# Causal attention on one core: four heads weighed in a row, diagonal masks in quarters of the array

## The chip, the cores and the metric

One core of a Trainium2 chip runs the whole program. The time is the device time of one execution, in microseconds; the time of a kernel is the median of its runs. The kernel before ran three times: 2082.1, 2084.21 and 2092.12 us, median 2084.21.

## What is computed

The reference has four layers on an input `x` of 4 batches by 1024 positions by 128: window attention (stage a in the kernel), gated linear attention with routes (stage b), causal attention with a short-term memory (stage c), and a mixture of experts (stage d). The change is in stage c alone. Of that stage, cut to the part that matters:

```python
B, L, D, H = (4, 1024, 128, 16); d = 8      # 16 heads of 8 columns
scores = jnp.einsum('bhid,bhjd->bhij', q, k) * scale
causal_mask = jnp.triu(jnp.full((Ll, Ll), -10000.0, dtype=scores.dtype), 1)
attn = jax.nn.softmax(scores + causal_mask, axis=-1)
y_softmax = jnp.einsum('bhij,bhjd->bhid', attn, v)
# a scan over positions gives y_stp; a gate mixes y_softmax and y_stp
```

## The kernel before, in words

**Units and items.** Stage c (`causal`, L990) works on units: one batch and one group of four heads, 16 units in all. Every engine walks the same list of items, written by a planner, `causal_order` (L855), and takes from it what is its own. The kinds that matter here are these.

- `M` (L1092): scores with query rows on the output's 128 partitions, for two heads at a time in the two halves of a two-bank PSUM buffer. VectorE takes the row maxima of them (L1261). A unit has 20 M.
- `S` (L1113): the negative maxima, turned, which then go into the operands of the next kind.
- `W` (L1120): the scores again, key rows on the partitions, the maxima already subtracted, for two heads (index `i` is the pair, `r` the head in it). ScalarE makes the weights from them with one exponential (L1375) into one of four SBUF buffers `c_probs`. A unit has 12 steps (`KEY_STEPS`, a chunk of 512 queries by 128 key rows) and so 24 W.
- `V` (L1139): weights times values (8 columns and a column of ones) for the two heads of one W, accumulated in one of two PSUM banks `acc`. Its matmuls are float32, with 9 output columns each; head `h` writes partitions from `32 * h` on, so the four heads of a group use four 32-column strips of the array. A unit has 24 V.
- `A` copies a finished chunk out of `acc` (L1381).

**Masks.** A tile of scores that holds a part of the diagonal gets the mask added by the array: a matmul of a scaled unit matrix (`half_rows`) with a matrix of 0 and -100 (`causal_row` for M, L1106 to L1111; `causal_col` for W, L1131 to L1137). Each constant is stored on 64 rows, twice, since the operands of the two heads lie in rows 0 to 63 and 64 to 127. A mask matmul reads 64 rows and writes all 128 output partitions; the first pair of matmuls serves output partitions 0 to 63 and adds zeros to the others, the second pair the other way round. So a diagonal pair of score matmuls is followed by four mask matmuls, of 128, 128, 64 and 64 columns (M) or 64, 64, 128 and 128 (W).

**What sets the order.** The scores of M, S and W and some side items share three PSUM buffers in turn (`ring`); PE waits for a buffer until the engine that reads its last content is done (`pe_wait_free`, L1010). The planner keeps a clock for PE, ScalarE and VectorE, with a price for each kind of item (`times`, L911). It puts W and V in their fixed order and lets M of later units go ahead of them where PE would not be held up (`put_ahead`, L960). V of a W is put three W later (`late`, L978). ScalarE's exponential into a buffer waits for the V that read this buffer four W before (L1374). Side items (the next batch's preparation, the short-term memory's scans, which take VectorE, ScalarE and POOL, and the finish of the batch before) are hung on fixed steps.

**Stages a and b** also appear in the rows: L500 and L524 are stage a's scores (up to 64 rows by 64 columns of the array), L459 its masks (64 by 64), L540 its values: 16 float32 matmuls for a block, in four 32-column strips and two halves of 64 rows. L1063 is stage c's first gate matmul, two matmuls into the same 64 columns. L1910 and L1864 are two groups of stage b with 64 and 128 output columns.

Of the kernel before, what the change touches and what calls it, by code (L numbers as in the profile page):

```python
# [13 lines left out]
P = 128  # L14
BANK = 512
EPS = 1e-5
HEADS, HD = 16, 8
# [47 lines left out]
def constant_columns():  # L65
# [13 lines left out]
        "half_rows": np.concatenate([r % 64 == c, r % 64 + 64 == c], 1) * 100.0,  # L79
# [37 lines left out]
def build(nc, x_in, packed, x_out, place, batches, T, known):  # L117
# [7 lines left out]
    with ctx:  # L125
# [729 lines left out]
        def causal_order():  # L855
# [55 lines left out]
            def times(item):  # L911
# [4 lines left out]
                if item[0] in "WV":  # L916
# [3 lines left out]
                    if item[0] == "V":  # L920
                        return 0.02 + 0.00103 * cols, (), 0
# [7 lines left out]
            def begin(item):  # L929
                t = clock["P"]  # L930
                if times(item)[2]:
                    t = max(t, free[0])
                return max(t, made[item[1:]]) if item[0] == "V" else t
# [36 lines left out]
            for u in units:  # L970
                for k, (c, j) in enumerate(KEY_STEPS):
                    for i in range(2):
# [17 lines left out]
        def causal():  # L990
# [49 lines left out]
            def pe_program():  # L1040
# [3 lines left out]
                for item in order:  # L1044
# [47 lines left out]
                    elif kind == "M":  # L1092
# [6 lines left out]
                        for i in range(per):  # L1099
                            pair = (g * GROUP + h0) // 2 + i  # L1100
                            o = [ps[:, r * BANK + i * width:r * BANK + (i + 1) * width] for r in range(2)]
                            for r in range(2):
                                mm = nc.tensor.matmul(o[r], qs[half(r, SCORE), pair, n * P:(n + 1) * P],  # L1103
                                                      ks[half(r, SCORE), pair, a:c], start=True, stop=not diag)
# [15 lines left out]
                    elif kind == "W":  # L1120
# [7 lines left out]
                        for r in range(2):  # L1128
                            mm = nc.tensor.matmul(ps[:, r * BANK:r * BANK + cols], ks[half(r, SHIFT), pair, j * P:(j + 1) * P],  # L1129
                                                  qs[half(r, SHIFT), pair, a:a + cols], start=True, stop=not diag)  # L1130
                        if diag:  # L1131
                            for r in range(2):
                                nc.tensor.matmul(ps[:, r * BANK:r * BANK + 64], w3["half_rows"][half(r, 64), 0:P],
                                                 w3["causal_col"][half(r, 64), 0:64], start=False, stop=False)
                            for r in range(2):
                                mm = nc.tensor.matmul(ps[:, r * BANK:r * BANK + P], w3["half_rows"][half(r, 64), P:2 * P],  # L1136
                                                      w3["causal_col"][half(r, 64), 64:64 + P], start=False, stop=True)  # L1137
                        mm.then_inc(c_key_scored.up(item), 1)
                    elif kind == "V":  # L1139
                        _, b, g, c, j, i = item  # L1140
# [6 lines left out]
                        if j == 0 and i == 0 and ci >= 2:  # L1147
# [1476 lines left out]
```

## Time and profile before

| what | value |
|---|---|
| median of three runs | 2084.21 us |
| the profiled execution's own time | 2081.97 us |
| its span | 2080.6 us |
| mean granted PE clock | 0.936 |
| instructions | 45291 |
| stage c | about 1058 to 1775 us |

A row of the profile names the line, the engine, the operation and the tiles, with the shape of a matmul as rows*columns of the stationary operand and the moving operand's partitions x columns. `busy` counts the time in which at least one such instruction is shown at work.
### The profile page before, as it was taken

Reading aid. Unit: us, or ns where it says so; the run is one execution under the profiler, and the core shown is the slowest. Engines: PE = TensorE matmul, PEld = TensorE weight load, DVE = VectorE, ACT = ScalarE, POOL = GpSimd, SP = SyncE. Lnnn points to the kernel's source line nnn. Section 1 sums busy time; section 2 is a strip of 40 time slices with the busy share of each in tenths; the row PEclk is TensorE's granted clock in tenths of the full one; section 3 lists DMA queues with packets and bytes.
Section 4 is the critical chain, followed back from the end, with each engine's and each line's share of the span. In section 5 each row is a group of like instructions: output and inputs, shape, how many; then the busy total and the mean of one; then the engine's idle time right before and its main releaser. Section 6 shows DMA issues by size and latency. Waiting matters only on the chain.

```text
span 2080.6 us, 45291 instructions
## 1 busy us (share of the span) xinstructions
PE 1812.6 (87%) x19452; PEld 1056.7 (51%) x19472; DVE 1295.3 (62%) x2096; ACT 1134.7 (55%) x1720; POOL 660.3 (32%) x468
## 2 busy tenths in 40 slices
PE   4688879999999999999658899799889988598799
PEld 2456646776677677677522324233333423355465
DVE  5566536666666666666566776586677663555544
ACT  2365647667666766766315676566566665222221
POOL 5220004342343434235504442544444344000000
PEclk8899969999999999999858999899999999799999
DMA  6754000000000000000161532252262220000000
GB/s 166 215 132 96 7 9 1 2 1 1 2 2 1 1 2 2 1 2 2 73 148 42 161 77 50 88 137 63 82 143 62 62 63 21 0 11 6 6 11 11
DMA packets 38361, 102.08 MB, mean 49 GB/s; under 512 B 3856, under 2 KB 12176, under 8 KB 34704
## 3 DMA queue, kind: packets, MB, share of 16 engines
q1 hardware_dynamic: 38160, 99.18, 18.5%
q8 instruction: 153, 2.51, 0.5%
q14 instruction: 48, 0.39, 0.1%
HBM read 66.93 MB, written 31.46 MB: 47 GB/s over the span
## 4 chain that ended last, share of the span: by engine, by line
PE 56%; DVE 20%; issue 8%; ACT 5%; POOL 4%; DMA 1%; POOLq 0%; DVEq 0%; SPq 0%; ACTq 0%
PE accs L1153 8%; DVE arena L1261 4%; PE ring L1870 3%; PE accs L1934 3%; PE ring L2364 3%; PE ring L2366 3%; PE accs L2333 3%; PE ring L1896 3%; PE ring L1129 2%; PE ring L1103 2%; DVE arena L1271 2%; PE ring L1864 2%; PE ring L1835 2%; DVE arena L2023 1%; DVE arena L2063 1%
## 5 line engine op out<-in xcount | busy, mean ns | idle before, releaser
L1261 DVE TENSOR_REDUCE arena<-ring 128x2 f32<-128x1024 f32 (+2 forms) x320 | 346.1, 1112 | 148.1 <-PE ring L1110 97.2
L1375 ACT ACTIVATE arena<-ring 128x1024 f32<-128x1024 f32 (+3 forms) x384 | 304.3, 808 | 174.4 <-PE ring L1136 139.0
L1153 PE MATMUL accs<-arena 128*9 128x512 f32 (+3 forms) x1536 | 322.2, 500 | 0.0
L1129 PE MATMUL ring<-arena 51*128 51x512 bf16 (+3 forms) x768 | 133.5, 342 | 26.7 <-DVE arena L1261 14.8
L1103 PE MATMUL ring<-arena 48*128 48x512 bf16 (+3 forms) x768 | 131.5, 353 | 22.7 <-DVE arena L1261 10.0
L2248 POOL TENSOR_TENSOR arena<-arena 128x1280 f32<-128x1280 f32 x28 | 65.3, 2332 | 265.2 <-PE accs L1934 234.6
L1129 PEld LDWEIGHTS ring<-arena 51*128 51x128 bf16 x768 | 37.9, 94 | 207.0 <-issue 82.9
L2240 POOL TENSOR_TENSOR arena<-arena 128x512 f32<-128x512 f32 x112 | 138.9, 1272 | 10.2 <-DVE arena L2044 10.2
L2232 POOL TENSOR_TENSOR arena<-arena 128x1024 f32<-128x1024 f32 x32 | 75.6, 2364 | 190.2 <-DVE arena L2063 190.2
L2443 DVE TENSOR_TENSOR arena<-arena,ring 128x512 f32<-128x512 f32 x80 | 55.0, 688 | 122.7 <-PE ring L2366 112.2
L2493 ACT ACTIVATE arena<-ring 128x512 f32<-128x512 f32 x80 | 47.8, 597 | 147.0 <-PE ring L2364 147.0
L1538 POOL TENSOR_TENSOR arena<-arena 128x1024 f32<-128x1024 f32 x28 | 65.9, 2352 | 190.5 <-ACT arena L1388 147.9
L294 PE MATMUL ring<-weights_constants,xn 128*128 128x128 f32 x124 | 35.4, 379 | 84.1 <-DVE xn L278 52.6
L1271 DVE TENSOR_TENSOR_SCAN arena<-arena 128x1024 f32<-128x1024 f32 x32 | 79.5, 2484 | 34.5 <-POOL arena L1526 34.5
L2333 PEld LDWEIGHTS accs<-weights_large,arena 128*128 128x128 f32 x640 | 85.1, 193 | 29.2 <-issue 26.3
L2063 DVE TENSOR_TENSOR arena<-ring,arena 128x1024 f32<-128x1024 f32 x32 | 39.2, 1225 | 85.9 <-PE ring L1896 85.9
L1896 PE MATMUL ring<-arena 64*128 64x128 f32 x1024 | 91.7, 285 | 0.2
L1896 PEld LDWEIGHTS ring<-arena 64*128 64x128 f32 x1024 | 79.2, 187 | 19.5 <-issue 12.9
L2159 ACT ACTIVATE arena<-ring 128x1024 f32<-128x1024 f32 x32 | 32.8, 1024 | 100.7 <-PE ring L1835 100.7
L1996 DVE SCALAR_TENSOR_TENSOR arena<-ring,arena 128x1024 f32<-128x1024 f32 x32 | 39.2, 1225 | 76.0 <-ACT arena L2163 76.0
L1103 PEld LDWEIGHTS ring<-arena 48*128 48x128 bf16 x768 | 38.3, 97 | 94.9 <-issue 34.8
L2333 PE MATMUL accs<-weights_large,arena 128*128 128x128 f32 x640 | 85.0, 276 | 1.5 <-DVE arena L2449 0.5
(334 smaller groups left out, 4365.5 us busy)
## 6 DMA issues: line engine op xcount, KB each, us to landing
arena<-whole_k SPq DMA_DIRECT2D x32, 512.0 KB, 4.6
arena<-whole_q SPq DMA_DIRECT2D x32, 512.0 KB, 6.2
arena<-a_scratch_q SPq DMA_DIRECT2D x16, 384.0 KB, 6.9
arena<-a_scratch_k SPq DMA_DIRECT2D x16, 384.0 KB, 8.3
arena<-c_scratch_q SPq DMA_DIRECT2D x16, 384.0 KB, 8.2
arena<-c_scratch_k SPq DMA_DIRECT2D x16, 384.0 KB, 10.1
a_scratch_k<-arena SPq DMA_DIRECT2D x8, 512.0 KB, 3.9
c_scratch_k<-arena SPq DMA_DIRECT2D x8, 512.0 KB, 5.2
```

Of the source, the lines that this page charges most:

```text
L1103: mm = nc.tensor.matmul(o[r], qs[half(r, SCORE), pair, n * P:(n + 1) * P], ks[half(r, SCORE), pair, a:c], start=True, stop=not diag)
L1129: mm = nc.tensor.matmul(ps[:, r * BANK:r * BANK + cols], ks[half(r, SHIFT), pair, j * P:(j + 1) * P], qs[half(r, SHIFT), pair, a:a + cols] ...
L1153: mm = nc.tensor.matmul(acc[ci % 2][32 * h:32 * h + HD + 1, a - c * BANK:BANK], c_values[b % 2][:, j, r * HEADS // 2 + 2 * g + i, :], weig ...
L1261: nc.vector.tensor_reduce(dst, src, AX.X, ALU.max, negate=True).then_inc(c_max_taken.up(item), 1)
L1271: nc.vector.tensor_tensor_scan(sk[:, :], c_retain[:, j:j + 1].to_broadcast([P, T]), sk[:, :], 0.0, ALU.mult, ALU.add).then_inc(c_state_mad ...
L1375: nc.scalar.activation(view(c_probs[wi % 4]), view(ps), ACT.Exp).then_inc(c_weights_made.up(item), 1)
L1538: nc.gpsimd.tensor_tensor(sq[:, :], sk[:, :], sq[:, :], ALU.mult).then_inc(c_y_step.up((b, j)), 1)
L1896: mm = nc.tensor.matmul(ps[:, r * BANK + p * P:r * BANK + (p + 1) * P], k_[t % 2][half(r), p * P:(p + 1) * P], q_[t % 2][half(r), p * P:(p ...
L2232: nc.gpsimd.tensor_tensor(masked[0][:, :], masked[0][:, :], masked[1][:, :], ALU.add).then_inc(gla_joined.up(t), 1)
L2240: nc.gpsimd.tensor_tensor(pair_cols(q2m[t % 2][:, r, :]), pair_cols(q2[t % 2][:, :]), hot_b[:, r * P:(r + 1) * P].unsqueeze(1).to_broadcas ...
L2248: nc.gpsimd.tensor_tensor(state_mid[:, :, :, :].rearrange("p a r d -> p (a r) d"), state[:, :, :, :].rearrange("p a r d -> p (a r) d"), fa ...
L2333: mm = nc.tensor.matmul(total[:, n * P:(n + 1) * P], hid[index[item] % 3][:, n * P:(n + 1) * P], w("d_down", f * P, (f + 1) * P), start=f ...
```

## The change

It does four things. In the planner, and in PE's program, a V is one item for all four heads of a step: its eight records follow each other, and it waits for the weights of both pairs. It is put behind both W of the next step (the list `late` holds one step). Its planned price is 0.00205 us per column in place of two items of 0.02 + 0.00103 per column. Each mask matmul writes only the 64 output partitions that it is for: a 64-column stationary operand and an output of 64 partitions, four matmuls for the four pairs of input half and output half. Waits of other engines on V are on the one item.

```diff
-        "half_rows": np.concatenate([r % 64 == c, r % 64 + 64 == c], 1) * 100.0,
+        "half_rows": (r % 64 == c[:, 0:64]) * 100.0,
...
-                        return 0.02 + 0.00103 * cols, (), 0
+                        return 0.00205 * cols, (), 0
...
-                return max(t, made[item[1:]]) if item[0] == "V" else t
+                return max(t, made[item[1:] + (1,)]) if item[0] == "V" else t
...
-                        late.append(("V", *u, c, j, i))
-                        if len(late) > 3:
-                            item = late.pop(0)
-                            put_ahead(item)
-                            put(item)
-                            if item[4:] == ((item[3] + 1) * BANK // P - 1, 1):
-                                sums.append(("A", *item[1:4]))
+
+                    late.append(("V", *u, c, j))
+                    if len(late) > 1:
+                        item = late.pop(0)
+                        put_ahead(item)
+                        put(item)
+                        if item[4] == (item[3] + 1) * BANK // P - 1:
+                            sums.append(("A", *item[1:4]))
...
                             if diag:
-                                for r in range(2):
-                                    nc.tensor.matmul(o[r][:, width - P:width], w3["half_rows"][half(r, 64), 0:P],
-                                                     w3["causal_row"][half(r, 64), 0:P], start=False, stop=False)
-                                for r in range(2):
-                                    mm = nc.tensor.matmul(o[r][:, width - 64:width], w3["half_rows"][half(r, 64), P:2 * P],
-                                                          w3["causal_row"][half(r, 64), P:P + 64], start=False, stop=True)
+
+                                for h, first, cols in ((0, width - P, slice(0, P)), (1, width - 64, slice(P, P + 64))):
+                                    for r in range(2):
+                                        mm = nc.tensor.matmul(o[r][half(h, 64), first:width], w3["half_rows"][half(r, 64), 0:64],
+                                                              w3["causal_row"][half(r, 64), cols], start=False, stop=True,
+                                                              skip_group_check=True)
...
                         if diag:
-                            for r in range(2):
-                                nc.tensor.matmul(ps[:, r * BANK:r * BANK + 64], w3["half_rows"][half(r, 64), 0:P],
-                                                 w3["causal_col"][half(r, 64), 0:64], start=False, stop=False)
-                            for r in range(2):
-                                mm = nc.tensor.matmul(ps[:, r * BANK:r * BANK + P], w3["half_rows"][half(r, 64), P:2 * P],
-                                                      w3["causal_col"][half(r, 64), 64:64 + P], start=False, stop=True)
+                            for h, last, columns in ((0, 64, slice(0, 64)), (1, P, slice(64, 64 + P))):
+                                for r in range(2):
+                                    mm = nc.tensor.matmul(ps[half(h, 64), r * BANK:r * BANK + last],
+                                                          w3["half_rows"][half(r, 64), 0:64], w3["causal_col"][half(r, 64), columns],
+                                                          start=False, stop=True, skip_group_check=True)
...
-                        pe.wait_ge(c_weights_made, ("W", *item[1:]))
-                        weights = c_probs[w_index["W", b, g, c, j, i] % 4]
-                        for r in range(2):
-                            h = 2 * i + r
-                            mm = nc.tensor.matmul(
-                                acc[ci % 2][32 * h:32 * h + HD + 1, a - c * BANK:BANK],
-                                c_values[b % 2][:, j, r * HEADS // 2 + 2 * g + i, :],
-                                weights[:, r * BANK:r * BANK + (c + 1) * BANK - a],
-                                start=j == 0, stop=j == (c + 1) * BANK // P - 1, skip_group_check=True)
+                        pe.wait_ge(c_weights_made, ("W", *item[1:], 1))
+                        for i in range(2):
+                            weights = c_probs[w_index["W", b, g, c, j, i] % 4]
+                            for r in range(2):
+                                h = 2 * i + r
+                                mm = nc.tensor.matmul(
+                                    acc[ci % 2][32 * h:32 * h + HD + 1, a - c * BANK:BANK],
+                                    c_values[b % 2][:, j, r * HEADS // 2 + 2 * g + i, :],
+                                    weights[:, r * BANK:r * BANK + (c + 1) * BANK - a],
+                                    start=j == 0, stop=j == (c + 1) * BANK // P - 1, skip_group_check=True)
...
-                            ac.wait_ge(c_weighed, ("V", *w_items[wi - 4][1:]))
+                            ac.wait_ge(c_weighed, ("V", *w_items[wi - 4][1:5]))
```

## Rows read from the trace of the kernel before

**Rows 1.** The page: busy time of each engine over the span.

```profile
PE 1812.6 (87%) x19452; PEld 1056.7 (51%) x19472; DVE 1295.3 (62%) x2096; ACT 1134.7 (55%) x1720; POOL 660.3 (32%) x468
```

**Rows 2.** Stretches of the causal stage; columns are named in the first line.

```profile
core 0: us, PE busy (x) PEld busy (x) DVE busy (x) ACT busy (x) POOL busy (x), PEclk, DMA share, GB/s
1058.00:1089.00 31.00, 19.44 (x172) 8.66 (x172) 26.70 (x28) 1.01 (x1) 3.32 (x5) 0.50 0.42 85
1089.00:1144.00 55.00, 48.01 (x398) 15.99 (x398) 38.18 (x51) 29.57 (x38) 21.23 (x18) 0.80 0.22 52
1300.00:1352.00 52.00, 40.95 (x322) 14.77 (x318) 30.38 (x31) 27.77 (x33) 29.88 (x22) 0.87 0.28 86
1352.00:1404.00 52.00, 49.21 (x508) 16.89 (x502) 41.82 (x37) 33.28 (x44) 21.99 (x14) 1.00 0.60 139
1404.00:1456.00 52.00, 50.53 (x478) 20.07 (x476) 36.13 (x42) 32.45 (x45) 21.67 (x17) 1.00 0.26 63
1612.00:1664.00 52.00, 51.51 (x506) 21.30 (x502) 35.68 (x43) 32.43 (x45) 20.92 (x13) 1.00 0.25 62
1089.00:1760.00 671.00, 610.62 (x5530) 219.29 (x5531) 448.27 (x478) 415.05 (x526) 294.43 (x198) 0.95 0.32 83
```

**Rows 3.** Chain of waits from 1196 to 1248 us, shares by line.

```profile
by line: PE accs L1153 38.1%; PE ring L1129 11.4%; PE ring L1103 10.7%; DVE arena L1261 9.8%; DVE arena L1271 8.5%; issue 7.5%; ACT arena L1375 7.4%; PE ring L1136 1.9%; PE ring L1107 1.9%; PE ring L1117 1.9%; PE ring L1133 1.1%; PE ring L1
```

**Rows 4.** Timeline of PE: start, us, engine, line, operation, out<-in, count.

```profile
1403.71 0.38 PE L1103 MATMUL ring<-arena 48*128 48x512 bf16 x2
1403.93 0.22 PE L1107 MATMUL ring<-bf_causal_row,bf_half_rows 64*128 64x128 bf16 x2
1403.99 0.19 PE L1110 MATMUL ring<-bf_causal_row,bf_half_rows 64*128 64x64 bf16 x2
1404.11 1.03 PE L1153 MATMUL accs<-arena 128*9 128x512 f32 x4
1405.07 0.28 PE L1129 MATMUL ring<-arena 51*128 51x256 bf16 x2
```

**Rows 5.** Groups of L540 (one block), L1063 (two matmuls), L1153 (one block): busy, mean ns.

```profile
L540 PE MATMUL ring<-arena 64*9 64x128 f32 x32 | 0.6, 270 | 0.0
...
L1063 PE MATMUL ring<-xnT,weights_small 128*64 128x512 f32 x4 | 1.9, 605 | 0.0
...
L1153 PE MATMUL accs<-arena 128*9 128x512 f32 x4 | 1.0, 594 | 0.0
```

**Rows 6.** Groups by shape, 1089 to 1760 us: busy us, mean ns | idle before.

```profile
L1153 PE MATMUL accs<-arena 128*9 128x512 f32 x768 | 204.2, 610 | 0.0
...
L1136 PE MATMUL ring<-bf_causal_col,bf_half_rows 64*128 64x128 bf16 x512 | 57.4, 218 | 0.0
L1153 PE MATMUL accs<-arena 128*9 128x384 f32 x256 | 52.5, 488 | 0.0
...
L1153 PE MATMUL accs<-arena 128*9 128x256 f32 x256 | 39.5, 392 | 0.0
L1153 PE MATMUL accs<-arena 128*9 128x128 f32 x256 | 26.3, 288 | 0.0
```

**Rows 7.** Timeline of PE in stages a and b, where the layout changes in columns.

```profile
157.13 0.41 PE L500 MATMUL ring<-arena 48*64 48x128 bf16 x16
157.47 0.65 PE L540 MATMUL ring<-arena 64*9 64x128 f32 x32
158.04 0.41 PE L459 MATMUL ring<-bf_win_col,ident 64*64 64x512 bf16 x4
...
429.22 0.65 PE L1910 MATMUL ring<-arena 128*64 128x256 f32 x4
429.81 0.61 PE L1864 MATMUL ring<-arena 128*128 128x136 f32 x3
```

**Rows 8.** Groups of VectorE and ScalarE, 1089 to 1760 us; idle before them last.

```profile
L1261 DVE TENSOR_REDUCE arena<-ring 128x2 f32<-128x1024 f32 (+2 forms) x295 | 320.7, 1115 | 138.7 <-PE ring L1110 88.0 <-PE ring L1103 49.4
L1375 ACT ACTIVATE arena<-ring 128x1024 f32<-128x1024 f32 (+3 forms) x384 | 304.3, 808 | 174.4 <-PE ring L1136 139.0 <-PE ring L1129 34.2
```

More of the change, by code:

```diff
@@ L1103, in pe_program @@
                                 mm = nc.tensor.matmul(o[r], qs[half(r, SCORE), pair, n * P:(n + 1) * P],
-                                                      ks[half(r, SCORE), pair, a:c], start=True, stop=not diag)
+                                                      ks[half(r, SCORE), pair, a:c], start=True, stop=not diag,
+                                                      skip_group_check=True)
                             if diag:
-                                for r in range(2):
-                                    nc.tensor.matmul(o[r][:, width - P:width], w3["half_rows"][half(r, 64), 0:P],
-                                                     w3["causal_row"][half(r, 64), 0:P], start=False, stop=False)
-                                for r in range(2):
-                                    mm = nc.tensor.matmul(o[r][:, width - 64:width], w3["half_rows"][half(r, 64), P:2 * P],
-                                                          w3["causal_row"][half(r, 64), P:P + 64], start=False, stop=True)
+                                for h, first, cols in ((0, width - P, slice(0, P)), (1, width - 64, slice(P, P + 64))):
+                                    for r in range(2):
+                                        mm = nc.tensor.matmul(o[r][half(h, 64), first:width], w3["half_rows"][half(r, 64), 0:64],
+                                                              w3["causal_row"][half(r, 64), cols], start=False, stop=True,
+                                                              skip_group_check=True)
                         mm.then_inc(c_row_scored.up(item), 1)
@@ L1129, in pe_program @@
                             mm = nc.tensor.matmul(ps[:, r * BANK:r * BANK + cols], ks[half(r, SHIFT), pair, j * P:(j + 1) * P],
-                                                  qs[half(r, SHIFT), pair, a:a + cols], start=True, stop=not diag)
+                                                  qs[half(r, SHIFT), pair, a:a + cols], start=True, stop=not diag,
+                                                  skip_group_check=True)
                         if diag:
-                            for r in range(2):
-                                nc.tensor.matmul(ps[:, r * BANK:r * BANK + 64], w3["half_rows"][half(r, 64), 0:P],
-                                                 w3["causal_col"][half(r, 64), 0:64], start=False, stop=False)
-                            for r in range(2):
-                                mm = nc.tensor.matmul(ps[:, r * BANK:r * BANK + P], w3["half_rows"][half(r, 64), P:2 * P],
-                                                      w3["causal_col"][half(r, 64), 64:64 + P], start=False, stop=True)
+                            for h, last, columns in ((0, 64, slice(0, 64)), (1, P, slice(64, 64 + P))):
[3 more added lines that the diff above has]
+                                                          start=False, stop=True, skip_group_check=True)
                         mm.then_inc(c_key_scored.up(item), 1)
                     elif kind == "V":
-                        _, b, g, c, j, i = item
+                        _, b, g, c, j = item
                         a = first_query(c, j)
@@ L1146, in pe_program @@
                         pe.wait_ge(c_cleared, ("ones", 1))
-                        if j == 0 and i == 0 and ci >= 2:
+                        if j == 0 and ci >= 2:
                             pe.wait_ge(c_copied, ci - 2)
-                        pe.wait_ge(c_weights_made, ("W", *item[1:]))
-                        weights = c_probs[w_index["W", b, g, c, j, i] % 4]
-                        for r in range(2):
-                            h = 2 * i + r
-                            mm = nc.tensor.matmul(
-                                acc[ci % 2][32 * h:32 * h + HD + 1, a - c * BANK:BANK],
-                                c_values[b % 2][:, j, r * HEADS // 2 + 2 * g + i, :],
-                                weights[:, r * BANK:r * BANK + (c + 1) * BANK - a],
-                                start=j == 0, stop=j == (c + 1) * BANK // P - 1, skip_group_check=True)
+                        pe.wait_ge(c_weights_made, ("W", *item[1:], 1))
[8 more added lines that the diff above has]
+                                    start=j == 0, stop=j == (c + 1) * BANK // P - 1, skip_group_check=True)
                         mm.then_inc(c_weighed.up(item), 1)
@@ L1242, in dve_program @@
                         if b >= 2:
-                            dv.wait_ge(c_weighed, ("V", b - 2, GROUPS - 1, *KEY_STEPS[-1], 1))
+                            dv.wait_ge(c_weighed, ("V", b - 2, GROUPS - 1, *KEY_STEPS[-1]))
                         nc.vector.tensor_tensor(
@@ L1377, in act_program @@
                         _, b, g, c = item
-                        ac.wait_ge(c_weighed, ("V", b, g, c, (c + 1) * BANK // P - 1, 1))
+                        ac.wait_ge(c_weighed, ("V", b, g, c, (c + 1) * BANK // P - 1))
                         if b:
```

## The prediction

> **What bounds the kernel now.** I read the page's sums first, then stretches of the causal stage, then the chain, then single matmuls. TensorE is busy for 87% of the span [rows 1], and the change touches one stage only, from about 1058 to 1760 us. From 1089 us on, where key rows are weighed, PE shows 610.6 of 671 us busy, VectorE (DVE) 448 and ScalarE (ACT) 415; in the calm stretches PE shows 50.5 and 51.5 of 52 us at the full clock, near a batch's start 41 [rows 2]. The chain through one calm stretch spends 38% in the weighing matmuls of L1153 [rows 3]. So PE sets the pace there, and the question is how much of it the change frees and what takes over.
>
> A PE row must be read with its tail: a 512-column weighing record lasts 0.594 us, but four of them span 1.03, so the second two started 0.43 after the first two [rows 4, 5]. 0.43 is streaming, 0.16 is drain that the next matmul overlaps. Where neighbours use the array the same way, the next starts when the streaming ends (L1103 at 1403.71, its mask 0.22 later). Where they don't, it starts later: L1110 streams 0.03 from 1403.99 and L1153 begins at 1404.11, 0.09 late; L1153 streams 0.86 from 1404.11 and L1129 begins at 1405.07, 0.10 late [rows 4]. I call this a switch.
>
 Its size: records average 0.610, 0.488, 0.392 and 0.288 us for 512, 384, 256 and 128 columns, each with 0.165 of tail; with 192, 64, 64 and 64 pairs of heads and two record-times per pair, 192x2x0.445 + 64x2x(0.323+0.227+0.123) = 257 us [rows 6]. Half is **128 us** less.
>
> There are also 192 blocks instead of 384. Each now stands alone between scores [rows 4], so 192x(0.09+0.10) = **36 us** less of switching.
>
> **Part 2: masks of 64 output rows.** Now four mask matmuls over 128 output rows follow their scores with no switch and cost 0.06 + 0.03 = 0.09 us (1403.93 to 1403.99, then 0.03) [rows 4]. After, they are quarters of the array: all four stream together, 0.053 us for the longest, half the difference that 128 columns make in the averages of rows 6 (0.104 from 128 to 256, two passes). But the layout now differs from that of the scores (64 rows by 128 columns of the array against 64 by 64). Does a change of columns alone cost a switch? Yes by the nearest rows: from 48*64 to 64*9, L500's streaming ends at 157.13+0.41-0.16 = 157.38 and L540 begins at 157.47; back, L540 ends at 157.96 and L459 begins at 158.04; and from 64 to 128 columns over all rows L1910 ends at 429.71 and L1864 begins at 429.81 [rows 7]. All are 0.08 to 0.10. These bound it: 0 below (if scores and masks pass without a drain), 0.09 above each way. I take 0.09 in and 0.095 out, since no change of layout in these rows was free. There are 512 pairs with a diagonal (256 in M, 256 in W; the 512 records of L1136, two per pair, are W's [rows 6]). 512x(0.053+0.09+0.095-0.09) = 76 us more; where a block of values follows the mask its own switch is already counted, about 125 of the 192 blocks (two steps of three are diagonal): 12 off. Net **64 us** more; with free switches it would be 19 us less.
>
> **Part 3: the later wait.** A block waits for the exponentials of its second score. Behind it in PE's queue stand the next M and W, for which DVE and ACT wait. From that second score to the block PE has one block (0.96), two scores (0.22 to 0.5 each) and most often one or two M: 1.9 to 2.8 us. ACT needs at most two exponentials of 0.81 on average [rows 8], more for 512 columns, and a hand-over: 1.8 to 2.3 us. So the wait is 0 mostly and 0.3 where no M stands between, in the last unit. ACT's wait for a free buffer is for a block that stands two steps back: nothing. The planner's price of four heads (0.00205 per column) is twice its price of two, so it spreads M nearly as before; I cost the new order at 0, between -5 and +10. The narrower constant is loaded and cast in stage a under other work: 0. No DMA is moved, and nothing on SyncE's or POOL's queue.
>
> **The sum.** PE gets 128 + 36 - 64 = **100 us** less work. It can't all show. DVE's 448 us and ACT's 415 [rows 2] would fill 78% and 73% of 571 us, and scores take turns in three PSUM buffers. In the densest stretch DVE has 41.8 of 52 us [rows 2], which would be 95% of a stretch 15% shorter. On the other side, DVE waits 139 us for scores (L1110's and L1103's) and ACT 174 us [rows 8], so both have room, and the block that keeps scores waiting comes half as often at the same length. The calm stretches should give their share nearly whole, the batch starts half of it, and the densest ones less: I take two thirds, 64 us. The profiled execution took 2081.97 us: 2018. The median of the runs shown lies 2.2 above it: **2020 us**.
>
> **A rule against it.** Two heads of 512 columns take 1.03 us [rows 4], two record-times and a tail. The Trainium skill, "TensorE: Matmul & The Clock Gate", Part 3, says that matmuls start and end in program order ("strict FIFO"). By that rule a head's second record would hold back the next head's first: two heads would take three record-times, 1.45 us with the tail. The trace disagrees: they take two.
>
> **The rivals.**
> B, masks switch for free: a gain of 19 in place of a loss of 64, so 183 us of relief, but then DVE binds in more stretches; 95 to 100 us show: 1986. For: masks follow in the same row halves. Against: every change of columns in rows 7 cost 0.09. 13%.
> C, another engine takes over at once: DVE, or the order of three buffers, lets a third through, 33 us: 2051. For: DVE at 41.8 of 52. Against: its waits of rows 8. 14%.
> D, the slower side: four heads don't run together. Place: L1153. If a 512-column block streams 1.72 us (two and two), the 128 us are gone while the masks' 64 stay: 64-36 = 28 us slower, 2112. It decides from about 1.53 us of streaming per 512-column block on, where 128 shrinks to 28. Against: eight at a time in rows 5; for: those read half the rows each, and no row has four full-height streams. The extreme of D is that each head's second record holds back the next head's first: five record-times, 2.15 us where two pairs stream 1.72 now, so 257 us become 321, +64 + 64 - 36 = 92 us slower, 2176. 6% for both, of which 1% for the extreme. That extreme is what the skill's strict order gives; the trace disagrees already at two heads.
> E, the change doesn't do what it says: if the planner's new order or the later wait makes PE stall by 0.33 us at each of the 192 blocks, the 64 us are eaten: 2084. Against: the slack worked out in part 3. 4%.
> F, the clock: PE's granted share is 0.80 to 0.87 in the batch starts and 0.50 in the stretch before [rows 2], where PE sat idle more. If a PE that waits more runs a fifth of its remaining 511 us (611 - 100) at half the clock, 102 us come back: 2122. Against: the calm stretches stay at 1.00 with masks and waits in them. 3%.
>
> **How the numbers follow.** A, the forecast, has 60%, its own range 1995 to 2045 (four to nine tenths of the relief). 0.5% is 10.4 us, about what a measurement can tell from no change. Faster: A+B+C = 0.87; same: E = 0.04; slower: D+F = 0.09. The range takes in A and nearly all of B and C: 1980 to 2055.
>
> **What would show it.** L1153: 192 groups of eight records, 512 columns in about 1.05 us; about 1.9 is rival D. Masks: 64*64, four starts within 0.01 us, 0.09 after the score's streaming ends; no gap is rival B. PE busy in the stage falls below DVE's pace: calm stretches near 44 us for what took 52, with DVE at 85% or more. DVE's wait for PE should shrink from 139 us; if it stays while PE's wait for DVE grows, the ring is the bound (C). Above 2074 I am wrong in kind; below 1980 the masks' price was wrong.

## The result and the profile after

The changed kernel takes 2109.62 us (median of 4 runs, 2107.08 to 2112.47) against 2085.37 for the kernel before. The ratio is 1.0112, with a 95% interval from 1.0082 to 1.0142: **1.1% slower**, clear of the noise, where 3.1% faster was forecast. The range ended at 2055. The profiled execution took 2112.47 us, its span is 2111.2.

The page of the changed kernel: busy times [rows 1], and the slices of the span with the granted clock.

```profile
PE 1817.4 (86%) x19452; PEld 1051.2 (50%) x19472; DVE 1289.1 (61%) x2096; ACT 1130.4 (54%) x1720; POOL 658.2 (31%) x468
...
PEclk8899969999999999999857779769878988799999
```

PE's sum is 5 us more than before. The clock row shows the first surprise: five slices at 7 and one at 6 between 1108 and 1785 us, where the stage changed by this work lies. The page of the kernel before has two slices at 8 there and 9 in all others:

```profile
PEclk8899969999999999999858999899999999799999
```

The stage in one row, from its first W score to its last weighing matmul (columns as in [rows 2]):

```profile
1094.00:1785.00 691.00, 603.63 (x5492) 210.83 (x5492) 436.40 (x467) 408.98 (x523) 286.04 (x196) 0.81 0.32 80
```

The same stage took 662 us before, 1089 to 1751:

```profile
1089.00:1751.00 662.00, 605.29 (x5497) 214.44 (x5498) 441.63 (x468) 414.08 (x524) 288.78 (x196) 0.95 0.33 84
```

The stage is 29 us longer, and PE shows the same 604 us of busy time. But PE got 0.81 of its clock in place of 0.95 (0.815 and 0.952 with one digit more). The granted clock in the traces has two levels, 1.2 and 2.4 GHz, so twice the missing share is the time at 1.2 GHz: 256 us of the stage after, 63 us before.

**Did the four heads run together?** The timeline of PE in two places, the first at the full clock and the second at half (columns as in [rows 4]; the last brackets give a wait and its releaser):

```profile
1618.45 0.23 PE L1131 MATMUL ring<-arena 51*128 51x128 bf16 x2 [0.76 <-DVE arena L1264]
...
1619.87 0.39 PE L1131 MATMUL ring<-arena 51*128 51x512 bf16 x2
1620.19 0.25 PE L1137 MATMUL ring<-bf_causal_col,bf_half_rows 64*64 64x64 bf16 x4
1620.37 0.39 PE L1104 MATMUL ring<-arena 48*128 48x512 bf16 x2
...
1624.21 1.04 PE L1156 MATMUL accs<-arena 128*9 128x512 f32 x8
1625.19 0.28 PE L1131 MATMUL ring<-arena 51*128 51x256 bf16 x2
```

```profile
1404.69 1.90 PE L1156 MATMUL accs<-arena 128*9 128x512 f32 x8
1406.52 0.40 PE L1131 MATMUL ring<-arena 51*128 51x256 bf16 x2
```

Yes: eight records of 512 columns last 1.04 us, where four did before [rows 4]. At half the clock the same block lasts 1.90. A reader who sees only the second row would take it for rival D, four heads in two turns. It isn't: the clock of the stretch tells them apart. The block at 1404.69 lies in a stretch with a granted clock of 0.50 (second row; columns as in [rows 2]):

```profile
1387.00:1391.00 4.00, 4.00 (x42) 2.41 (x38) 0.73 (x4) 0.98 (x4) 0.00 (x0) 0.92 1.01 193
1391.00:1411.00 20.00, 17.45 (x150) 5.03 (x143) 12.87 (x12) 8.05 (x13) 7.98 (x7) 0.50 0.64 136
1411.00:1418.00 7.00, 5.18 (x63) 2.17 (x61) 5.46 (x5) 5.67 (x8) 0.90 (x1) 0.96 0.02 6
```

**Masks.** The score that starts at 1619.87 has streamed its 512 columns (0.22 us) at 1620.09; its masks begin at 1620.19, 0.10 late; the next score begins 0.18 after them. A pair's masks cost 0.28 us of PE, against 0.09 before.

The same by shape, weighing matmuls of the stage (busy us, mean ns, idle before; compare [rows 6]):

```profile
L1156 PE MATMUL accs<-arena 128*9 128x512 f32 x768 | 125.1, 729 | 1.8 <-ACT arena L1378 1.8
...
L1156 PE MATMUL accs<-arena 128*9 128x384 f32 x256 | 32.8, 590 | 0.0
...
L1156 PE MATMUL accs<-arena 128*9 128x256 f32 x256 | 22.8, 432 | 0.0
...
L1156 PE MATMUL accs<-arena 128*9 128x128 f32 x256 | 15.3, 310 | 0.5 <-ACT arena L1378 0.5
```

By the prediction's own formula they stream 96x2x0.564 + 32x2x(0.425+0.267+0.145) = 162 us, from 257. Half would have been 128.5; each record is longer on average, 729 ns for 610, because a part of the blocks ran at half the clock, as the one of 1.90 us did.

VectorE's maxima and ScalarE's exponentials wait more, not less ([rows 8] had 138.7 and 174.4), and PE waits more for the maxima before its W scores: 31.5 us, from 14.8. By the prediction's own sign, this is the ring of three buffers and not PE alone.

```profile
L1264 DVE TENSOR_REDUCE arena<-ring 128x2 f32<-128x1024 f32 (+1 forms) x294 | 321.0, 1115 | 174.5 <-PE ring L1111 99.5 <-PE ring L1104 73.8
L1378 ACT ACTIVATE arena<-ring 128x1024 f32<-128x1024 f32 (+3 forms) x384 | 300.7, 809 | 190.8 <-PE ring L1137 154.4 <-PE ring L1131 34.2
L1131 PE MATMUL ring<-arena 51*128 51x512 bf16 (+3 forms) x768 | 142.1, 376 | 43.2 <-DVE arena L1264 31.5 <-ACT arena L1335 4.7 <-ACT arena L1378 3.1
```

and in the kernel before:

```profile
L1129 PE MATMUL ring<-arena 51*128 51x512 bf16 (+3 forms) x768 | 133.5, 342 | 26.7 <-DVE arena L1261 14.8 <-DVE arena L1244 6.0 <-ACT arena L1332 4.9
```

The chain through a stretch at the full clock, 1612 to 1664 us, was led by the weighing matmuls before (first row) and is led by VectorE after (second row):

```profile
by line: PE accs L1153 41.6%; PE ring L1129 14.4%; DVE arena L1261 8.3%; PE ring L1103 8.0%; PE ring L1164 7.3%; DVE arena L1271 4.2%; PE ring L1180 3.8%; PE ring L1182 3.4%; PE ring L1172 2.8%; PE ring L1136 2.3%; PE ring L1107 1.7%; PE ri
by line: DVE arena L1264 31.1%; PE accs L1156 19.9%; PE ring L1104 9.6%; PE ring L1131 9.5%; DVE arena L1274 8.5%; PE ring L1137 5.5%; PE ring L1167 3.9%; PE ring L1111 3.9%; PE ring L1084 3.7%; PE ring L1078 2.0%; ACT arena L1361 2.0%; iss
```

Every engine waits more for another. That fits a loop better than one bound engine; e9, e10 and e12 below test it.

### The profile page after: what moved, and what is told of

The parts are those of the page before. It is cut to its first block, busy times and chain, and to the rows that moved or that the text cites. A ratio compares the mean times of both kernels' runs of the same rounds, so it can differ in the third digit from the quotient of the medians.

```text
span 2111.2 us, 45102 instructions
## 1 busy us (share of the span) xinstructions
PE 1817.4 (86%) x19452; PEld 1051.2 (50%) x19472; DVE 1289.1 (61%) x2096; ACT 1130.4 (54%) x1720; POOL 658.2 (31%) x468
## 4 chain that ended last, share of the span: by engine, by line
PE 55%; DVE 22%; issue 7%; ACT 4%; POOL 4%; DMA 1%; POOLq 0%; DVEq 0%; SPq 0%
DVE arena L1264 7%; PE accs L1156 5%; PE ring L1873 3%; PE accs L1937 3%; PE ring L2367 3%; PE ring L1104 3%; PE ring L2369 3%; PE accs L2336 3%; PE ring L1131 3%; PE ring L1899 3%; DVE arena L1274 2%; PE ring L1838 2%; PE ring L1867 2%; DVE arena L2026 1%; DVE arena L2066 1%
## 5 line engine op out<-in xcount | busy, mean ns | idle before, releaser
L1156 PE MATMUL accs<-arena 128*9 128x512 f32 (+3 forms) x1536 | 196.0, 587 | 2.3 <-ACT arena L1378 2.3
L1104 PE MATMUL ring<-arena 48*128 48x512 bf16 (+3 forms) x768 | 151.0, 391 | 40.1 <-DVE arena L1264 11.6
L1131 PE MATMUL ring<-arena 51*128 51x512 bf16 (+3 forms) x768 | 142.1, 376 | 43.2 <-DVE arena L1264 31.5
L1131 PEld LDWEIGHTS ring<-arena 51*128 51x128 bf16 x768 | 36.6, 96 | 159.8 <-DVE arena L1264 85.4
L1104 PEld LDWEIGHTS ring<-arena 48*128 48x128 bf16 x768 | 38.1, 96 | 120.4 <-DVE arena L1264 32.2
```

The costliest lines, as they stand in the source:

```text
L1156: mm = nc.tensor.matmul(acc[ci % 2][32 * h:32 * h + HD + 1, a - c * BANK:BANK], c_values[b % 2][:, j, r * HEADS // 2 + 2 * g + i, :], weig ...
```

## The experiments

Each run stands beside runs of the kernel before on the same chip. To read them I split PE's time in the stage into three, from the start of every matmul. **Streaming** is columns over the clock granted at that moment (a float32 record streams its columns twice, as in the prediction). If the next matmul starts later than that and its layout differs, up to 0.105 us is **switch**. The rest is **wait**. The three add up to the stage. The expectations of e5, e8 and e10 were written with an earlier count; it differs from this table by up to 22 us.

```
kernel                     ratio to before    stage  stream switch wait  clock
before                     1                   661    494     79    88   0.95
after (the change)         1.0112 +-0.0030     691    423    134   134   0.81
e1  change, old masks      0.9803 +-0.0019     624    401     44   178   0.88
e2  before, new masks      1.0244 +-0.0017     717    487    163    68   0.94
e3  e1, pairs in series    1.0197 +-0.0016     705    508     44   153   0.93
e4  change, M twice        1.0201 +-0.0030     700    461    132   107   0.87
e5  e1, M twice            0.9865 +-0.0035     640    448     44   148   0.92
e6  e1, other prices       0.9803 +-0.0036     624    403     44   178   0.88
e8  change, M and W twice  1.0260 +-0.0033     728    507    129    93   0.91
e9  e1, half maxima        0.9533 +-0.0027     578    384     44   149   0.92
e10 change, half maxima    0.9829 +-0.0032     633    395    134   104   0.87
e11 two heads, new place   1.0163 +-0.0031     691    489     78   125   0.95
e12 before, half maxima    0.9782 +-0.0021     628    486     79    64   0.97
e13 before, later wait     1.0000 +-0.0018     659    492     79    88   0.96
e14 e3, own waits          1.0221 +-0.0022     705    510     44   151   0.93
e15 e1, own waits          0.9794 +-0.0021     623    403     44   175   0.88
```

The clock is that of the stage's row in each trace; five such rows are copied below, each beside its run.

### Parts of the change alone: e1, e2, e3

**e1_quads** is the changed kernel with the mask blocks and the constant of before:

```diff
-                                for h, first, cols in ((0, width - P, slice(0, P)), (1, width - 64, slice(P, P + 64))):
-                                    for r in range(2):
-                                        mm = nc.tensor.matmul(o[r][half(h, 64), first:width], w3["half_rows"][half(r, 64), 0:64],
...
+                                for r in range(2):
+                                    nc.tensor.matmul(o[r][:, width - P:width], w3["half_rows"][half(r, 64), 0:P],
...
```

> The change without its masks: four heads in a row with the new order, masks as before. T1 (the granted clock falls because blocks of four heads thin out TensorE's work, whoever makes the gaps): clock over the causal stage still below before's 0.95, at 0.85 to 0.90, and a time of 2060 to 2090. T2 (the clock falls because the masks change the array's layout some 800 times more often): clock 0.93 or more over the stage, 192 blocks of 1.03 us, time 1980 to 2010.

Measured: 2045.55 us, 2.0% faster than before. The clock is T1's; the time lies between the two ranges.

```profile
1087.00:1710.00 623.00, 498.03 (x5492) 203.02 (x5488) 435.65 (x467) 406.03 (x523) 286.40 (x196) 0.88 0.36 89
```

**e2_masks** is the kernel before with the change's masks (the same edit the other way).

> The masks alone, blocks of two heads and the order as before. Both theories: about 64 to 76 us of layout changes more on TensorE, so slower, 2130 to 2160 at an unchanged clock. T1: the clock of the stage stays within 0.03 of before. T2: it falls to 0.85 or less and the time goes above 2160. If layout changes cost nothing: 2065 to 2085.

Measured: 2136.19 us, 2.4% slower, at a clock of 0.94, as T1 had it.

```profile
1087.00:1804.00 717.00, 677.87 (x5486) 222.08 (x5488) 441.53 (x468) 415.65 (x523) 287.84 (x196) 0.94 0.31 77
```

So the masks cost 64 us on top of the four heads (2109.6 - 2045.6) and 50 on the kernel before. Their price on PE is read from e2, whose clock is nearly that of before: switches +84, streaming -7, **77 us**, where 64 was forecast. 56 of them lengthen the stage. The masks alone turn a gain of 2% into a loss of 1%.

**e3_order** is e1 with the second pair of heads in the strips of the first, so that the two pairs run one after the other. The sums of heads 2 and 3 are added to those of heads 0 and 1, and the memory that this leaves unwritten is set to one.

```diff
-                                    acc[ci % 2][32 * h:32 * h + HD + 1, a - c * BANK:BANK],
+                                    acc[ci % 2][32 * r:32 * r + HD + 1, a - c * BANK:BANK],
```

> As the run with four heads in a row and masks as before, but the second pair of heads writes the same two 32-column strips as the first, so that two heads run at a time; the sums of heads 2 and 3 are left out and strips 2 and 3 keep ones. It has the new order and half the layout changes of blocks, without four heads at once. T1: blocks of 1.9 us at the full clock, clock as before (0.93 to 0.95), time 2050 to 2075 (36 us of layout changes less). A rival, that the new order or the later wait itself costs: 2085 to 2110. T2 says the same as T1 here.

Measured: 2126.74 us, above all that I had expected (2050 to 2075, or 2085 to 2110). The timeline of its PE shows the block at full length:

```profile
1410.70 1.89 PE L1155 MATMUL accs<-arena 128*9 128x512 f32 x8
1412.52 0.39 PE L1130 MATMUL ring<-arena 51*128 51x512 bf16 x2
```

PE streams 14 us more than before, partly at the lower clock, and saves 35 of switches, just as forecast. Yet the stage is 44 us longer, since waits grow by 65. Two blocks of 0.86 us at two places, joined to one of 1.7 at one place, cost more by far than 36 us of switches bring. This run doesn't part the place of the block, which the planner's new order sets, from its length. From e3 to e1 the blocks shrink to half: streaming -107, waits +25, and 81 us off the time.

### The clock: e4, e5, e8

If PE's sparser work is why the clock fell, useless work should bring the clock back. **e4_more_work** issues each M score twice in the changed kernel (same operands, same result); **e5_quads_more_work** does so in e1; **e8_both_twice** doubles the W scores too.

```diff
-                            for r in range(2):
+                            for r in (0, 1, 0, 1):
```

> The changed kernel with each row-score matmul (M) issued twice, the first result overwritten: some 60 us more of streaming at the full clock. T1: the granted clock of the stage rises from 0.83 to above 0.92, and the time stays within 25 us of the changed kernel's 2110 although 60 us of work are added. T3 (the clock falls because four full-height float32 streams at once are too much for the chip): clock no higher than 0.83 and a time of 2150 to 2190.

> Four heads in a row, masks as before, and each row-score matmul (M) issued twice: 60 us more of streaming than the same kernel without it (2046, of which 159 us of the stage at half the clock and 176 us of waits of TensorE). T1 (the clock falls where TensorE's work is thin): time at half the clock falls to 60 to 110 us, and the time stays at 2035 to 2060, since the work goes into waits and the faster clock pays it back. If the clock had another cause: half-clock time of 150 us or more and 2075 to 2105.

> The changed kernel with both score matmuls (M and W) issued twice: 120 us more of streaming at the full clock. T1: the time at half the clock falls again, from 264 us (once) and 192 (M twice) to 130 or less, the time rises by 10 to 40 over M twice, 2135 to 2165. If half-clock time stays near 190 or rises, thin work is not its cause.

Measured: 2127.9, 2062.23 and 2146.32 us. The rows of the stage in e4 and e8:

```profile
1098.00:1798.00 700.00, 636.49 (x6195) 219.11 (x6191) 438.37 (x467) 411.81 (x523) 286.14 (x196) 0.87 0.31 79
```

```profile
1099.00:1827.00 728.00, 675.72 (x6962) 234.95 (x6959) 438.38 (x467) 415.06 (x524) 286.55 (x196) 0.91 0.30 76
```

The granted clock rises with the work, 0.81 to 0.87 to 0.91, and from 0.88 to 0.92 in e5. The second M scores are some 57 us of streaming at full clock (176 pairs of 512 columns at 0.22, 58 each of 0.16, 0.11 and 0.05). In e4 streaming grew by 38, the waits shrank by 27 and the time grew by 18. So the direction is shown: more work on PE raises its clock. T3, that four full-height streams at once are too much for the chip, does not stand: e4 and e8 have the same blocks of four heads and a higher clock. The sizes were less than expected: e4 was to reach 0.92 or more, and e5's time is 2 us above its range. The clock never came back whole, and extra work never paid for itself. The Trainium skill, "TensorE: Matmul & The Clock Gate", Part 1, says that the gate passes the full clock by how busy PE has lately been; the three runs agree, with the granted shares above. But PE's busy column does not tell it: the stage has 604 us of it at a clock of 0.81 and 605 at 0.95, because records get longer as the clock gets lower.

### The planner's prices: e6

**e6_prices** is e1 with prices that the rows of PE give: 0.00042 us per score column for 0.00077, 0.09 per pair's mask for 0.15, and 0.19 + 0.00167 per column for a weighing block.

> Four heads in a row, masks as before, and the planner's prices of M, W and V set to what the rows show at the full clock (0.42 ns per column of scores, 0.09 us per mask, 0.19 us and 1.67 ns per column for a block). If the order written for slower scores is what holds TensorE up (waits of 176 us), the time falls to 2015 to 2035; if the waits come from VectorE and the three buffers, it stays within 10 us of 2046.

Measured: 2050.27 us, ratio 0.9803 as e1. Nothing follows from better prices here; all three numbers of PE's account stay where they were, so the planner's prices are not what makes PE wait.

### What paces the stage: e9, e10, e12

These take VectorE's maxima over half the columns only (the maxima are of other numbers, the rest of the work stays), in e1, in the changed kernel and in the kernel before:

```diff
+                        if per == 1:
+                            src = ps[:, :].rearrange("p (r c) -> p r c", r=2)[:, :, 0:width // 2]
...
-                            src = src.rearrange("p r (i c) -> p r i c", i=per)
+                            src = src.rearrange("p r (i c) -> p r i c", i=per)[:, :, :, 0:width // 2]
```

> Four heads in a row, masks as before, and VectorE takes each row maximum over half of the columns only; the maxima over the other half are left out, 150 us less work on VectorE. If VectorE and the buffers that it holds took the relief over (TensorE waits 176 us in this kernel without the edit), the time falls by 30 us or more, to 1995 to 2015, and TensorE's waits fall below 130 us. If the order or TensorE itself binds, it stays within 12 us of 2046.

> The changed kernel with the same half maxima (the maxima over the other half of the columns are left out). Here TensorE streams 445 us, switches 122 and waits 125 of 691. If TensorE at its lower clock with the masks' layout changes binds, the time falls by less than 20 us, to 2090 to 2108; if VectorE binds here too, it falls by 30 us or more, below 2080.

> The kernel before with each row maximum taken over half of the columns (the other half is left out), 150 us less on VectorE. The prediction's reading, that TensorE alone sets the pace: within 15 us of before, 2070 to 2085. If the loop of scores, maxima and three buffers sets it together with TensorE (as the same edit showed on the changed kernel, 60 us): 2020 to 2050.

Measured: 1988.13, 2050.02 and 2037.05 us: 57, 60 and **47 us** less. e9 gained more than expected, though its waits are 149 us and not below 130. e12 was the control of the prediction's reading: with PE alone as the bound, relief on VectorE would have been worth 15 us at most. Its stage and its maxima:

```profile
1078.00:1706.00 628.00, 591.57 (x5492) 211.27 (x5488) 302.93 (x465) 412.69 (x523) 293.18 (x196) 0.97 0.34 89
```

```profile
L1263 DVE TENSOR_REDUCE arena<-ring 128x2 f32<-128x512 f32 (+2 forms) x292 | 182.7, 636 | 239.1 <-PE ring L1110 145.9 <-PE ring L1103 92.1
```

Streaming -8, waits -24, and 11 us are gained ahead of the stage. (e9 has the least work of all: VectorE shows 307 us of 577, ScalarE 399, PE streams or switches for 428, and PE still waits 149.) No engine is full. Work goes round a loop: a score needs one of three buffers, the maximum or exponential that reads it frees the buffer, and the scores stand in one queue with the weighing blocks. Each part of the loop counts in part. The clock of the stage rose as well, without any work added to PE: 0.95 to 0.97 (e12), 0.88 to 0.92 (e9), 0.81 to 0.87 (e10).

How much it counts differs from place to place. I split the same traces by unit, from one unit's first W to the next one's. In the calm units 2, 3, 6, 7, 10 and 11 PE waits 16 of 210 us before, and e12 takes 7 off: there PE nearly sets the pace. Units 1, 5 and 9 hold 44 us of waits in 184, and e12 takes 13 off. Four heads at a time (e1) take 47 us of work from PE in the six calm units, but its waits grow to 45 and 18 us show. In units 1, 5 and 9 they take 22 us of work and nothing shows: 186 us, 68 of them waits.

### The place of the blocks or the later wait: e11, e13, e14, e15

**e11_pairs_apart** keeps e1's order and later wait, but holds the second pair back behind the next M or W, so that blocks are of two heads again:

```diff
+                    if held and (kind == "att" or kind == "V" or (held[0] != item and last_kind in ("M", "W"))):
+                        pe_weigh(held.pop(0), 1)
...
+                        pe_weigh(item, 0)
+                        held.append(item)
```

> The new order and the new wait, masks as before, but the second pair of heads of a block is issued behind the next M or W, so that pairs never stand together: blocks of two heads of 0.86 us, 384 of them, with the layout changes of before. The run with both pairs in the same strips, one block of 1.7 us, took 2127 with 36 us less of layout changes. If the long block is what starves the other engines there: 2080 to 2100, TensorE's waits near before's 85 us. If the new order or the later wait is: 2110 to 2150, waits of 120 us or more.

Measured: 2115.82 us, 1.6% more than before. By what was expected that spoke for the new order or the later wait (2110 to 2150, waits of 120 us or more). Its PE streams and switches as before did (489 + 78), at the same clock; only the waits are 37 us longer.

```profile
1403.77 1.03 PE L1052 MATMUL accs<-arena 128*9 128x512 f32 x4
1404.73 0.39 PE L1150 MATMUL ring<-arena 51*128 51x512 bf16 x2
1405.05 1.03 PE L1052 MATMUL accs<-arena 128*9 128x512 f32 x4
```

This looked like the price of the new order, and it isn't only that. The view of waits shows (waiting line, releaser, us in total, times, longest):

```profile
ACT arena L1390 <- PE accs L1052: 146.6, 102, 3.5
```

In all others this wait doesn't occur. The edit made the second pair so late that exponentials waited for its buffer. So e11 leaves the term open, and three more runs went to it. **e13_before_later_wait** puts only the later wait into the kernel before; **e14_serial_own_waits** and **e15_quads_own_waits** take it out of e3 and e1.

```diff
-                        pe.wait_ge(c_weights_made, ("W", *item[1:]))
+                        pe.wait_ge(c_weights_made, ("W", *item[1:5], 1))
```

```diff
-                        pe.wait_ge(c_weights_made, ("W", *item[1:], 1))
                         for i in range(2):
+                            pe.wait_ge(c_weights_made, ("W", *item[1:], i))
```

> The kernel before, order and blocks untouched, but the first pair's weighing waits for the exponential of the second pair too. e11 (two-head blocks in the new order, with the later wait) was 34 us slower than before, but in it ScalarE's exponentials waited 147 us for weighing matmuls that the edit itself had put late, so it does not say what the change's order costs. Theory W (the later wait costs): 2105 to 2120, PE's waits of the stage grow from 85 us to 110 or more. Theory N (where the blocks stand costs, not the wait): 2080 to 2092, within 0.3% of before, waits 80 to 90, since three scores lie between a block and the exponentials that it needs.

> e3 (both pairs of a step in a row, in the same strips, so one after the other; 2126.7) with each pair waiting for its own exponential only. As in e3 the sums of heads 2 and 3 are added to those of heads 0 and 1. Theory W: 15 to 30 us less than e3, 2097 to 2112. Theory N: as e3 within 0.4%, 2118 to 2134; then the 41 us by which e3 exceeds before, with 36 us of switches saved, are the price of blocks of 1.7 us standing where scores are wanted.

> e1 (four heads at a time, masks as before; 2045.6) with each pair waiting for its own exponential only. Theory W: 2015 to 2032. Theory N: within 0.4% of e1, 2037 to 2054, clock of the stage 0.88 again.

Measured: 2084.15, 2128.85 and 2041.87 us. Theory N holds three times. The later wait costs nothing (1.0000 in e13, no difference in the other two beyond what such runs tell apart). What costs in e3 is the place of the block or its length; no run here tells which.

## Why the prediction was wrong

The account of the stage beside the forecast, both as after less before:

```
                    forecast   measured
streaming             -147       -71      (4 heads -128, masks 512x(0.053-0.09) = -19)
switches               +47       +55      (-36, +512x(0.09+0.095) = +95, -12)
PE's work             -100       -16
waits                  +36       +46      (forecast: a third of the relief doesn't show)
stage                  -64       +30
```

**Part 1, the mechanism: right.** Four heads run together, 1.04 us for eight records of 512 columns; the 36 us of switches went as forecast (79 to 44 in e1). Rival D's mechanism did not occur, though its 2112 us is nearly what was measured: a right number for a wrong reason. The prediction's "rule against it" took each record for a matmul of its own. If a float32 matmul counts as one, program order is not broken here: four records start within 0.02 us, four more 0.43 later, and they end in that order.

**Part 2: right in kind, somewhat small.** 77 us of PE's work in e2 for the 64 forecast. The switch on the way out is nearer 0.12 than 0.095, and what the change of layout costs was rightly taken from [rows 7].

**Rival F, the clock: the step that failed most.** It had 3%, and the sum has no term for it: all its streaming is priced at the full clock. In the same count with all columns at 2.4 GHz the stage streams 471 us before and 336 after, 135 less where 147 was forecast. But the lower level added 23 us before and adds 87 after. These 64 us are the largest part of the 94 us between the stage forecast and the one measured; streaming adds 12 more, switches 8, waits 10. Half-clock time went from 63 to 256 us. The argument against F was that calm stretches stay at 1.00 with masks and waits in them. In the calm units PE waited little (16 of 210 us) and streamed 166, and that is what the change thins out (142 of 224). Rival F's own condition, PE at half clock for a fifth of its work, was exceeded (87 of 336 us), though its price was 64 us and not 102. That the clock would give back all 64 us isn't shown: in a loop part of it would turn into waits. Why the masks take the clock from 0.88 to 0.81 in the packed kernel and leave it at 0.94 in e2 stays open.

**Part 3, "I cost the new order at 0": failed, and not by the wait.** The wait that the prediction worked out is indeed free (e13, e15). What it left out shows in e3: with the same streaming per head as before, waits grow by 65 us and the stage by 44, when two blocks are joined to one in the new order. That is 0.34 us for each of 192 blocks, the stall of rival E (4%). A likely cause is that the joined block keeps PE away from the scores for longer at a time, but place and length of the block were not parted. How much of this is left when the block is short again, as in e1, no run shows cleanly; e11 tried and brought a wait of its own.

**"PE sets the pace there", and two thirds: failed.** In e1 PE's work fell by 128 us (streaming 93, switches 35) and the time by 41: a third, which is the share of rival C (14%). The calm stretches were read rightly for the kernel before, but of their share, to show "nearly whole", 18 of 47 us showed; of the units 1, 5 and 9 nothing did, where half was taken. e12 shows what was missed: VectorE at 442 of 662 us with waits of 137 for scores looked like room, yet a cut of 139 us in its busy time took 47 off the kernel.

**The sum put together from runs:** serial pairs at the change's place and with its wait +41 (e3), four heads at once -81 (e1), masks +64 (the change): +24, which adds up by construction. By the forecast's own two thirds, the four heads with their switches were to show 109 us (of 164) and the masks to cost 43 (of 64). Measured: 41 (the first two terms) and 64.

**What beats both kernels** is e1, the four heads without the new masks: 2.0% faster than before (0.9785 to 0.9822). e15 is its equal.

## What to carry to other kernels

Before counting relief on TensorE as time, cut another engine's work in the same loop and see if the kernel moves; a busy share of nine tenths over a stage, tails included, hid 88 us of waits here, and where the waits are decides what relief is worth. A small matmul in its own layout between large ones costs two switches, here some 0.2 us a pair, more than its columns. And work packed tighter on TensorE may be granted a lower clock: read the granted clock of a packed trial before believing the sum.

## What the runs showed of the hardware

- Four float32 matmuls of 128 rows in four strips of 32 columns cost as much as two: 1.04 and 1.03 us for 512 columns. That all four read 128 rows did not hold them back.
- Layout changes cost 0.10 us in and up to 0.12 out even where the rows stay and only the columns go from 128 to 64 (L1131 to L1137 to L1104). The Trainium skill, "TensorEngine Tiling (Array Packing)", Key Properties, says that a change of tiling mode drains the engine; the rows agree, and give it this price.
- The granted clock of a stage fell from 0.95 to 0.88 with four heads at a time (e1; 0.93 in the same order with two heads at a time, e3) and to 0.81 with the masks between, though the same masks on the kernel before left it at 0.94 (e2). Doubled scores raised it again by 0.04 to 0.10.
